# A graph layer whose nodes are reordered so that each lane holds 36 consecutive ones, with column groups of 2048, 2560 and 392

## The chip, the core and the metric

One core of a Trainium2 chip runs the whole program. The metric is the device time of one execution in microseconds. The kernel before takes 252.86 us, the median of three runs (252.83 to 253.35).

## What is computed

```python
h = maximum(layernorm(x), 0)                      # x: 5000 x 64, float32
neighbors = adj @ h                               # adj: 5000 x 5000, float32
neighbors = neighbors / (num_neighbors[:, None] + 1e-7)
out = concat([h, neighbors], -1) @ fc_w.T + fc_b  # fc_w: 64 x 128
return x + relu(out)
```

The matrix adj holds 5000 x 5000 floats, 100 MB, and every element is used once. All else (x, the weights, the result) is 1.28 MB or less apiece.

## The kernel before, in words

The host hands over adj transposed and cut by columns into three tensors, adj_group0 to adj_group2. A row of such a tensor belongs to one source node, a column to one target node. The 5000 nodes are split into 40 tiles of up to 128; 512 nodes (four tiles, RUN) make a block, and lane p of a block holds its nodes 4p to 4p+3, so that one lane's part of a block is contiguous in memory. Nine full blocks (FULL) make 4608 nodes. The other 392 nodes are the tenth block, whose tiles 36, 37 and 38 hold 384 of them for the product, and 8 remaining nodes (REM) go by a small buffer, adj_rem. I write "row t" for the 128 source nodes of tile t: one load of four rows brings 128 lanes x 4 rows x the group's width.

**Prologue.** VectorE and ScalarE normalize x in five sets of eight tiles (normalize, L341 and following; ln_square, ln_std). TensorE turns each set (turn), multiplies it with both halves of the weights (weigh), ScalarE copies the half that adj will multiply into g_sb (copy_g), and VectorE adds the bias to the other half into out_sb (add_bias). Sets 1 to 4 are turned and weighed between products of the first group, at the rows in TURN_AFTER and WEIGH_AFTER.

**The stream.** SyncE's queue issues 35 loads of adj (load, L205 to L212), in order, into one buffer raw of 32768 floats per lane. The first two groups are 2048 columns wide, and their loads of four rows (4.19 MB) go through four slots. The third is 904 wide and uses nine smaller slots of the same buffer. A load waits on the count load_used, which TensorE raises by one after the last product of each load: load n of the wide groups waits until load n-4 has been used. For each row t TensorE multiplies g_sb[t] with the row's columns in two halves of the array at once (multiply, L478 to L486), and sums in PSUM: each bank of acc holds 2 x 512 target nodes, side 0 in lanes 0 to 63, side 1 in lanes 64 to 127. A float32 product is two matmul instructions, so a 2048-wide row is eight of them and a 904-wide row four.

**Counts.** num_neighbors is loaded in nine rows of 512 into every twelfth lane of nn, inverted at full size, and spread to all lanes by one matmul with a one-lane selector (pick) per side and set (spread, L467 to L475), after rows 31 to 35 of the first group. ScalarE copies the result into rnn_bc.

**Between groups.** When a group's sums are complete, VectorE scales them by the counts (scale), TensorE flips them back to node-major form between products of the next group (flip, at FLIP_AFTER), and VectorE adds the self part, applies relu and adds x (finish). ScalarE's queue stores a group's result (store).

**End.** The last group's bank is scaled in two halves, flipped onto a preloaded self part (preload_self, flip_last), finished in two halves (finish_last) and stored: the full block by ScalarE's queue, the last 392 nodes by SyncE's.

```python
if n >= WIDE_SLOTS:
    sp.wait_ge(load_used, loads_before(n))            # SyncE, before the load is issued
```

Of the kernel before, what the change touches and what calls it, by code (L numbers as in the profile page):

```python
# [7 lines left out]
ALU = mybir.AluOpType  # L8
# [8 lines left out]
WIDE_SLOTS = 4  # L17

REM_STEP = 4
NN_STEP = 12  # L20
# [4 lines left out]
P = 1  # L25
GROUPS = [(0, 2048, 0), (2048, 2048, 2), (4096, 904, 4)]
ALIGN = 1

LAST_STEPS = (4, 4, 4, 4, 4, 4, 2, 2, 2, 1)


def gnn_layer(nc, x, adj_groups, num_neighbors, fc_t, fc_b, out):

# [15 lines left out]
    LAST_W = N - TAIL0  # L49
    LAST_LANES = LAST_W // RUN  # L50
    PAD0 = LAST_LANES // 32 * 32
    assert 0 < REM <= 32 and TAIL_RUN == RUN - 1 and TILES % (2 * RUN) == 0 and LAST_W % RUN == 0
    G = len(GROUPS)
    BANKS = TILES // (2 * RUN)
    LAST = BANKS - 1
    BT = 2 * RUN
    WIDE = GROUPS[0][1]
    NARROW = GROUPS[-1][1]
    NARROW_SLOTS = WIDE_SLOTS * WIDE // NARROW

    def banks(g):
        first, w, b0 = GROUPS[g]
        return range(b0, b0 + -(-w // (2 * BLOCK)))

    def sides(g, b):

        first, w, _ = GROUPS[g]
        c = b * 2 * BLOCK - first
        return [(0, c, min(BLOCK, w - c)), (1, c + BLOCK, min(BLOCK, w - c - BLOCK))]
# [3 lines left out]
    for g in range(G):  # L73
        for m in range(FULL + 1):
            n = RUN if m < FULL else TAIL_RUN
            step = RUN if g < G - 1 else LAST_STEPS[m]
            LOADS += [(g, m, i, min(n, i + step)) for i in range(0, n, step)]
    FIRST_LOAD = [[ld[0] for ld in LOADS].index(g) for g in range(G)]
    NARROW0 = FIRST_LOAD[G - 1]

    def slot(n):

        if n < NARROW0:
            return n % WIDE_SLOTS, n % WIDE_SLOTS * RUN * WIDE, n // WIDE_SLOTS
        k = n - NARROW0
        return k % NARROW_SLOTS, k % NARROW_SLOTS * RUN * NARROW, k // NARROW_SLOTS

    def loads_before(n):

        if n < NARROW0:  # L90
            return n - WIDE_SLOTS + 1
        if n - NARROW0 >= NARROW_SLOTS:
            return n - NARROW_SLOTS + 1
        end = slot(n)[1] + RUN * NARROW - 1
        return max(k for k in range(NARROW0) if k % WIDE_SLOTS <= end // (RUN * WIDE) and
                   k % WIDE_SLOTS >= slot(n)[1] // (RUN * WIDE)) + 1

# [3 lines left out]
    SPREAD_AFTER = {(0, 31 + b): b for b in range(BANKS)}  # L101
# [3 lines left out]
    LN_OPS = 9  # L105

    with ExitStack() as ctx:
# [5 lines left out]

        raw = sb("raw", [LANES, WIDE_SLOTS * RUN * WIDE])
        adj_rem = sb("adj_rem", [LANES, WIDE])
# [3 lines left out]
        cen = sb("cen", [LANES, BT, F])  # L119
        h_pairs = [sb(f"h_pairs{i}", [LANES, BT, F]) for i in range(2)]  # L120
        ht = [sb(f"ht{i}", [LANES, BLOCK]) for i in range(2)]
        ht_rows = sb("ht_rows", [LANES, BLOCK])
        rnn_bc = sb("rnn_bc", [LANES, BANKS, RUN, LANES])
        sums = [sb(f"sums{i}", [LANES, RUN, LANES]) for i in range(2)]
        ht_rem = sb("ht_rem", [LANES, LANES])
        nn = sb("nn", [LANES, BLOCK])
        rnn = sb("rnn", [LANES, BLOCK])
        pick = sb("pick", [LANES, 2 * BANKS, HALF])
        w_both = sb("w_both", [2 * F, 2 * F])
        bias = sb("bias", [LANES, F])  # L130
        ident = sb("ident", [LANES, LANES])
        mean = sb("mean", [LANES, BT])
# [5 lines left out]
        acc = [ctx.enter_context(nc.psum_tensor(f"acc{b}", [LANES, BLOCK], F32)) for b in range(BANKS)]  # L138
        turned = ctx.enter_context(nc.psum_tensor("turned", [LANES, BLOCK], F32))
        y = [ctx.enter_context(nc.psum_tensor(f"y{s}", [LANES, BLOCK], F32)) for s in range(2)]  # L140

        x_cleared = sem("x_cleared")
        x_loaded = [sem("x_loaded_first"), sem("x_loaded_rest")]
# [4 lines left out]
        loaded_wide = [sem(f"loaded_wide{s}") for s in range(WIDE_SLOTS)]  # L148
        loaded_narrow = [sem(f"loaded_narrow{s}") for s in range(NARROW_SLOTS)]
# [6 lines left out]
        pad_cleared = sem("pad_cleared")  # L156
        pick_ready = sem("pick_ready")
        rem_cleared = sem("rem_cleared")
        rnn_chain = sem("rnn_chain")
        turned_done = sem("turned_done")  # L160
# [15 lines left out]
        def runs(v, r):  # L176
            return v.rearrange("(p i) f -> p (i f)", i=r)

# [3 lines left out]
        def tile_major(v):  # L182
            return v.rearrange("k (p i) -> k i p", i=RUN)

        def half_runs(v, k):

            return v[:, BT * LAST:TILES, :].rearrange("p (s k i) f -> p k s (i f)", s=2, k=2)[:, k, :, :]

        def half_sides(k):

            return y[k][:, 0:BLOCK // 2].rearrange("p (s j) -> p s j", s=2)
# [4 lines left out]
        def loaded(n):  # L196
            k, _, before = slot(n)
            return (loaded_wide if n < NARROW0 else loaded_narrow)[k], 16 * before + 16

        block = ctx.enter_context(nc.Block())  # L200

        @block.sync
        def _(sp):
            def load(n):
                g, m, i0, i1 = LOADS[n]  # L205
                w = GROUPS[g][1]
                if n >= WIDE_SLOTS:
# [32 lines left out]
        def _(act):  # L240
            def load_rem(g):
                w = GROUPS[g][1]
# [4 lines left out]
                act.dma_start(adj_rem[0:REM * REM_STEP:REM_STEP, 0:w], adj_groups[g][REM0:N, 0:w]  # L247
                              ).then_inc(rem_loaded, 16)
# [8 lines left out]
            def load_counts():  # L257
                act.wait_ge(nn_cleared, 1)
                m = 2 * BANKS - 1
                act.dma_start(nn[0:m * NN_STEP:NN_STEP, :], num_neighbors[0:TAIL0].rearrange("(m n) -> m n", n=BLOCK)  # L260
                              ).then_inc(nn_loaded, 16)
                act.dma_start(nn[m * NN_STEP:m * NN_STEP + 1, 0:LAST_W],
                              num_neighbors[TAIL0:N].rearrange("(m n) -> m n", m=1)).then_inc(nn_loaded, 16)

            def ln_square(b):
                act.wait_ge(ln_dve, LN_OPS * b + 3)
                nc.scalar.activation(out_sb[:, BT * b:BT * (b + 1), :], cen[:], ACT.Square).then_inc(ln_act, 1)  # L267
# [5 lines left out]
            def copy_turned(b):  # L273
# [3 lines left out]
                if b < LAST:  # L277
                    nc.scalar.activation(ht[b % 2][:], turned[:], ACT.Copy).then_inc(turned_copied, 1)  # L278
                else:

                    nc.scalar.activation(tile_major(ht_rows[HALF:LANES, :]),
                                         turned[HALF:LANES, :].rearrange("k (i p) -> k i p", i=RUN), ACT.Copy)

                    p0 = (REM0 - TAIL0) // RUN
                    nc.scalar.activation(
                        ht_rem[HALF:LANES, 0:REM * REM_STEP].rearrange("k (p i z) -> k p i z", i=RUN, z=REM_STEP)[:, :, :, 0],
                        turned[HALF:LANES, :].rearrange("k (i p) -> k p i", i=RUN)[:, p0:LAST_LANES, :], ACT.Copy)
                    nc.scalar.activation(ht[b % 2][:], turned[:], ACT.Copy).then_inc(turned_copied, 1)

            def copy_g(b):  # L290
                act.wait_ge(weighed, b + 1)
                for s in range(2):
                    t0 = BT * b + RUN * s
                    nc.scalar.activation(g_sb[:, t0:t0 + RUN, :],  # L294
                                         y[s][:].rearrange("p (i k) -> p i k", i=RUN)[:, :, F:2 * F],
                                         ACT.Copy).then_inc(g_copied, 1)

            def copy_spread(b):
                act.wait_ge(spread_done, b + 1)
                nc.scalar.activation(rnn_bc[:, b, :, :], tile_major(y[b % 2][:]), ACT.Copy).then_inc(spread_copied, 1)  # L300

            def store(g):
                t0 = banks(g)[0] * BT
                t1 = t0 + len(banks(g)) * BT if g < G - 1 else t0 + RUN
                act.wait_ge(out_ready, banks(g)[-1] + 1)
                act.dma_start(out[t0 * LANES:t1 * LANES, :].rearrange("(m p i) f -> p m (i f)", p=LANES, i=RUN),
# [273 lines left out]
```

## Time and profile before

| | before |
|---|---|
| median of 3 runs | 252.86 us |
| the profiled execution's own time | 253.62 us |
| its span in the profile | 251.8 us |
| adj loads | 35, in all 100 MB |
| mean rate of the DMA engines over the span | 408 GB/s |
| TensorE busy | 202.7 us (80%) |
| VectorE busy | 37.0 us (15%) |
| ScalarE busy | 15.7 us (6%) |

The span runs from the first instruction to the last on the core; the 1.8 us between span and time lie around it. Busy time tells how long an engine had something to do, not that the end waited for it. "DMA share" is the mean busy share of the core's 16 DMA engines in a stretch (values a little over 1 come from how packets are put into the stretches). A timeline row gives start, length, engine, line, output and inputs; what stands in brackets is the idle time before it and what ended it.

### The profile page before, as it was taken

To read this page: it belongs to the slowest core of one execution; us is meant where nothing else is said; L and a number is where in the kernel's file an instruction comes from. 1 tells how busy PE (TensorE), PEld (TensorE's weight loads), DVE (VectorE), ACT (ScalarE), POOL (GpSimd) and SP (SyncE) were. 2 spreads that over 40 slices of the span, in tenths; PEclk is the share of its full clock that TensorE was granted. 3 is DMA by queue.
4 is the path that set the end of the run, shared out by engine and by line. 5 is a ranking of instruction groups with operands and counts; after the bars stand their busy time and mean duration, and the time that the engine had idled before them with its cause. 6 is when DMAs were issued, how large, how long until landed. Compare 5 with 4: busy or idle time off the path is not lost.

```text
span 251.8 us, 2143 instructions
## 1 busy us (share of the span) xinstructions
PE 202.7 (80%) x956; PEld 74.5 (30%) x956; DVE 37.0 (15%) x78; ACT 15.7 (6%) x34; POOL 2.6 (1%) x8
## 2 busy tenths in 40 slices
PE   0409997797696997999599995985866999998994
PEld 0403342332231532333132331221221334443431
DVE  4650063336100010002002200000000001310002
ACT  3210112120120010200000000000000000000000
POOL 4000000000000000000000000000000000000000
PEclk9999999999999999999979998899999999999999
DMA  6899999999999999999999999999999999999971
GB/s 182 365 427 453 432 426 418 422 458 436 422 422 416 437 450 409 450 416 424 442 437 442 428 429 429 432 430 432 428 418 433 415 430 425 434 415 419 422 286 37
DMA packets 8156, 102.80 MB, mean 408 GB/s; under 512 B 1134, under 2 KB 3635, under 8 KB 4804
## 3 DMA queue, kind: packets, MB, share of 16 engines
q1 hardware_dynamic: 6448, 101.22, 94.3%
q10 hardware_dynamic: 1700, 1.46, 1.7%
q8 instruction: 7, 0.11, 0.2%
q14 instruction: 1, 0.01, 0.0%
HBM read 101.40 MB, written 1.28 MB: 408 GB/s over the span
## 4 chain that ended last, share of the span: by engine, by line
DMA 75%; PE 21%; SPq 1%; DVE 1%; issue 0%
DMA raw<-adj_group 75%; PE acc L484 20%; SPq L212 1%; PE acc L494 0%; DVE out_sb L414 0%; PE y L520 0%; SPq L221 0%; PE turned L445 0%; PE y L506 0%; DVE nn L337 0%; DVE sums L398 0%; DVE x_sb L338 0%; DVE warm L336 0%
## 5 line engine op out<-in xcount | busy, mean ns | idle before, releaser
L484 PE MATMUL acc<-raw,g_sb 128*64 128x512 f32 (+1 forms) x780 | 180.6, 601 | 36.0 <-DMA raw<-adj_group 35.8
L484 PEld LDWEIGHTS acc<-raw,g_sb 128*64 128x64 f32 x780 | 59.1, 140 | 146.4 <-issue 97.5
L398 DVE TENSOR_TENSOR sums<-acc,rnn_bc 128x512 f32<-128x512 f32 (+1 forms) x6 | 3.3, 597 | 118.8 <-PE acc L484 118.8
L445 PE MATMUL turned<-ident,h_pairs 128*128 128x128 f32 x20 | 3.7, 315 | 8.7 <-DVE h_pairs L367 8.7
L376 DVE TENSOR_TENSOR out_sb<-y,bias 128x256 f32<-128x256 f32 x10 | 3.8, 419 | 33.1 <-ACT g_sb L294 33.1
L459 PE MATMUL y<-w_both,ht 64*128 64x128 f32 (+1 forms) x80 | 7.6, 317 | 0.8 <-ACT ht L278 0.8
L459 PEld LDWEIGHTS y<-w_both,ht 64*128 64x128 f32 x80 | 6.3, 215 | 4.4 <-issue 4.4
L404 DVE TENSOR_TENSOR out_sb<-y,out_sb 128x512 f32<-128x512 f32 x4 | 2.8, 692 | 30.6 <-PE y L506 30.6
L354 DVE TENSOR_REDUCE var<-out_sb 128x8 f32<-128x512 f32 x5 | 3.4, 686 | 23.2 <-ACT out_sb L267 23.2
L445 PEld LDWEIGHTS turned<-ident,h_pairs 128*128 128x128 f32 x20 | 2.4, 155 | 11.9 <-issue 11.1
L494 PE MATMUL acc<-adj_rem,g_sb 128*64 128x512 f32 (+1 forms) x20 | 5.6, 582 | 0.0
L294 ACT ACTIVATE g_sb<-y 128x256 f32<-128x256 f32 x10 | 3.3, 380 | 32.5 <-PE y L459 19.4
L473 PE MATMUL y<-rnn,pick 128*64 128x512 f32 x20 | 5.1, 592 | 0.0
L300 ACT ACTIVATE rnn_bc<-y 128x512 f32<-128x512 f32 x5 | 3.0, 597 | 17.5 <-PE y L473 17.5
L278 ACT ACTIVATE ht<-turned 128x512 f32<-128x512 f32 x4 | 2.4, 597 | 26.6 <-PE turned L445 26.6
L348 DVE TENSOR_REDUCE mean<-x_sb 128x8 f32<-128x512 f32 x5 | 3.4, 680 | 2.4 <-DMA x_sb<-x 2.4
L352 DVE TENSOR_TENSOR cen<-x_sb,mean 128x512 f32<-128x512 f32 x5 | 3.5, 693 | 0.2
L360 DVE TENSOR_TENSOR cen<-cen,rstd 128x512 f32<-128x512 f32 x5 | 3.5, 692 | 0.2
L267 ACT ACTIVATE out_sb<-cen 128x512 f32<-128x512 f32 x5 | 3.1, 626 | 5.5 <-DVE cen L352 3.6
L385 DVE RECIPROCAL rnn<-nn 128x512 f32<-128x512 f32 x1 | 3.4, 3353 | 0.0
L407 DVE SCALAR_TENSOR_TENSOR out_sb<-out_sb,x_sb 128x512 f32<-128x512 f32 x4 | 2.8, 691 | 0.1
L506 PEld LDWEIGHTS y<-ident,sums 128*128 128x128 f32 x16 | 1.7, 141 | 3.2 <-issue 3.2
(36 smaller groups left out, 28.3 us busy)
## 6 DMA issues: line engine op xcount, KB each, us to landing
raw<-adj_group SPq DMA_DIRECT2D x18, 4096.0 KB, 31.4
raw<-adj_group SPq DMA_DIRECT2D x6, 1808.0 KB, 25.2
raw<-adj_group SPq DMA_DIRECT2D x2, 3072.0 KB, 29.3
raw<-adj_group SPq DMA_DIRECT2D x6, 904.0 KB, 25.4
raw<-adj_group SPq DMA_DIRECT2D x3, 452.0 KB, 17.6
out<-out_sb ACTq DMA_DIRECT2D x2, 512.0 KB, 28.9
x_sb<-x SPq DMA_DIRECT2D x1, 896.0 KB
x_sb<-x SPq DMA_DIRECT2D x1, 256.0 KB, 2.9
```

The costliest lines, as they stand in the source:

```text
L294: nc.scalar.activation(g_sb[:, t0:t0 + RUN, :], y[s][:].rearrange("p (i k) -> p i k", i=RUN)[:, :, F:2 * F], ACT.Copy).then_inc(g_copied, 1)
L348: nc.vector.tensor_reduce(mean[:], x_sb[:, t0:t1, :], AX_X, ALU.add).then_inc(ln_dve, 1)
L352: nc.vector.tensor_tensor(cen[:], x_sb[:, t0:t1, :], bcast(mean[:]), ALU.subtract).then_inc(ln_dve, 1)
L354: nc.vector.tensor_reduce(var[:], out_sb[:, t0:t1, :], AX_X, ALU.add).then_inc(ln_dve, 1)
L360: nc.vector.tensor_tensor(cen[:], cen[:], bcast(rstd[:]), ALU.mult).then_inc(ln_dve, 1)
L376: nc.vector.tensor_tensor(out_sb[:, t0:t0 + RUN, :], y[s][:].rearrange("p (i k) -> p i k", i=RUN)[:, :, 0:F], bias[:].unsqueeze(1).to_broa ...
L385: nc.vector.reciprocal(rnn[:], nn[:]).then_inc(rnn_chain, 1)
L445: last = nc.tensor.transpose(turned[:, i * LANES:(i + 1) * LANES], flat(h_pairs[b % 2][:, 2 * i:2 * i + 2, :]), ident[:])
L459: last = nc.tensor.matmul(y[s][:, c:c + (F if apart else 2 * F)], ht[b % 2][k, c:c + LANES], w_both[k, 0:F if apart else 2 * F], start=Tru ...
L473: last = nc.tensor.matmul(y[b % 2][s * HALF:(s + 1) * HALF, :], pick[:, 2 * b + s, :], rnn[:], start=True, stop=True, tile_position=(0, s ...
L484: last = nc.tensor.matmul(acc[b][s * HALF:(s + 1) * HALF, 0:width], g_sb[:, t, :], raw[:, c + c0:c + c0 + width], start=t == 0, stop=t == ...
L494: last = nc.tensor.matmul(acc[b][s * HALF:(s + 1) * HALF, 0:width], g_sb[:, CH, :], adj_rem[:, c0:c0 + width], start=False, stop=False, ti ...
```

## The change

The host orders the first 4608 nodes otherwise: lane p of the 128 holds the 36 consecutive nodes 36p to 36p+35, and block m takes from lane p the nodes 36p + 9i + m (i = 0 to 3). So x, the counts and the result of these nodes are each one contiguous run per lane. The last 392 nodes are laid out as two sides of 196, two nodes a lane in 98 lanes.

- **x** comes in by one DMA of 9216 bytes per lane and one of 98 lanes x 2 x 512 bytes. Normalizing, adding the bias and finishing read and write strided views of the new order.
- **Groups** are now 2048, 2560 and 392 columns wide. The second has two full banks and one of 2 x 256 columns, the third one bank of 2 x 196 columns, which reuses the PSUM bank named turned.
- **Loads in rings.** Row t of a group stands at place (RING[g][0] + t mod RING[g][1]) times the group's width in raw: 16 rows of 2048, 12 rows of 2560, or rows from place 20 on of 392. A load waits until every earlier load that overlaps its place has been used (loads_before). There are 37 loads. The last one of the first group (load 9, rows 36 to 38) stands at floats 8192 to 14335; the first of the second group (load 10, rows 0 to 3) at 0 to 10239.
- **Counts** are loaded with 36 per lane, inverted at that size, widened to 64 copies each in rnn_wide (VectorE), and spread by matmuls with the identity: 4 of 128 columns per set, and for the last set 12 of 64 or 98 columns.
- **End.** scale_last, flip_last and finish_last work on two pieces of 98 nodes x 2 sides. The bank before it is scaled into a zeroed cen and flipped with a doubled identity (ident_twice).

```diff
-GROUPS = [(0, 2048, 0), (2048, 2048, 2), (4096, 904, 4)]
-LAST_STEPS = (4, 4, 4, 4, 4, 4, 2, 2, 2, 1)
+P = 512
+GROUPS = [(0, 4, 0), (4, 5, 2), (9, 1, 5)]
+STEPS = [(4, 4, 4, 4, 4, 4, 4, 4, 4, 4), (4, 4, 4, 4, 4, 4, 4, 4, 2, 1), (4, 4, 4, 4, 4, 4, 4, 2, 2, 1)]
+RING = [(0, 16), (0, 12), (20, 60)]
...
+    def place(n):
+
+        g, m, i0, _ = LOADS[n]
+        return (RING[g][0] + (m * RUN + i0) % RING[g][1]) * WIDTH[g]
...
     def loads_before(n):
...
+        return max([k + 1 for k in range(n) if place(k) < place_end(n) and place(n) < place_end(k)] + [n - LANDINGS + 1, 0])
...
-    FLIP_AFTER = {(1, 7): 0, (1, 9): 1, (2, 7): 2, (2, 11): 3}
-    PRELOAD_AFTER = (2, 23)
+    FLIP_AFTER = {(1, 7): 0, (1, 9): 1, (2, 9): 2, (2, 13): 3, (2, 17): 4}
+    PRELOAD_AFTER = (2, 25)
...
-            load_x(0, 2).then_inc(x_loaded[0], 16)
-            load_x(2, FULL).then_inc(x_loaded[1], 16)
+            sp.dma_start(flat(x_sb[:, 0:ROWS, :]), x[0:TAIL0, :].rearrange("(p r) f -> p (r f)", r=ROWS)
+                         ).then_inc(x_loaded[0], 16)
...
             def spread(b):
...
-                for s in range(2):
-                    last = nc.tensor.matmul(y[b % 2][s * HALF:(s + 1) * HALF, :], pick[:, 2 * b + s, :], rnn[:],
-                                            start=True, stop=True, tile_position=(0, s * HALF))
+                if b < PAIRS:
+                    for i in range(RUN):
+                        t = i * FULL + 2 * b
+                        last = nc.tensor.matmul(y[b % 2][:, i * LANES:(i + 1) * LANES], flat(rnn_wide[:, t:t + 2, :]),
+                                                ident[:], start=True, stop=True)
...
             def flip_last():
-                for k in range(2):
-                    pe.wait_ge(scaled, LAST + k + 1)
-                    for i in range(2):
-                        last = nc.tensor.matmul(half_sides(k)[:, :, i * F:(i + 1) * F],
-                                                sums[LAST % 2][:, 2 * k + i, :], ident[:], start=False, stop=i == 1)
-                    last.then_inc(flipped, 1)
+                for i in range(2):
+                    pe.wait_ge(scaled, LAST + i + 1)
+                    nc.tensor.matmul(y[i][0:LAST_LANES, 0:2 * F], sums[0][:, i * LAST_LANES:(i + 1) * LAST_LANES],
+                                     ident[:], start=False, stop=True).then_inc(flipped, 1)
```

SyncE's queue before, the loads of x and of adj (sizes are lanes x floats):

```order
L215 DMA x_sb<-x 128x2x256
L215 DMA x_sb<-x 128x7x256
L221 DMA x_sb<-x 98x256 [waits x_cleared]
L212 DMA raw<-adj_group 128x8192 x4
L212 DMA raw<-adj_group 128x8192 [waits load_used] x5
L212 DMA raw<-adj_group 128x6144 [waits load_used]
L212 DMA raw<-adj_group 128x8192 [waits load_used] x9
L212 DMA raw<-adj_group 128x6144 [waits load_used]
L212 DMA raw<-adj_group 128x3616 [waits load_used] x6
L212 DMA raw<-adj_group 128x1808 [waits load_used] x6
L212 DMA raw<-adj_group 128x904 [waits load_used] x3
```

And with the change:

```order
L226 DMA x_sb<-x 128x2304
L229 DMA x_sb<-x 98x2x128 [waits x_cleared]
L224 DMA raw<-adj_group 128x8192 x4
L224 DMA raw<-adj_group 128x8192 [waits load_used] x5
L224 DMA raw<-adj_group 128x6144 [waits load_used]
L224 DMA raw<-adj_group 128x10240 [waits load_used] x8
L224 DMA raw<-adj_group 128x5120 [waits load_used] x2
L224 DMA raw<-adj_group 128x2560 [waits load_used] x3
L224 DMA raw<-adj_group 128x1568 [waits load_used] x7
L224 DMA raw<-adj_group 128x784 [waits load_used] x4
L224 DMA raw<-adj_group 128x392 [waits load_used] x3
```

One load of x is gone, and the adj loads stand one place earlier. The queue is in order: a load that waits holds back all behind it. The first 128x10240 load (load 10) waits for a load_used of 10, that is for the use of the 128x6144 load right before it; before the change it waited for a count of 7.

TensorE from row 31 to row 38 of the first group before (y is the spread counts, acc the sums):

```order
L484 MATMUL acc<-raw,g_sb 64x512 x16
L473 MATMUL y<-rnn,pick 64x512 x2
L484 MATMUL acc<-raw,g_sb 64x512 x4
...
L484 MATMUL acc<-raw,g_sb 64x512 x4
L473 MATMUL y<-rnn,pick 64x512 x2
L484 MATMUL acc<-raw,g_sb 64x512 x8
L494 MATMUL acc<-adj_rem,g_sb 64x512 x4
L484 MATMUL acc<-raw,g_sb 64x512 x36
```

And with the change:

```order
L544 MATMUL acc<-raw,g_sb 64x512 x16
L523 MATMUL y<-ident,rnn_wide 128x128 x4
L544 MATMUL acc<-raw,g_sb 64x512 x4
...
L544 MATMUL acc<-raw,g_sb 64x512 x4
L529 MATMUL y<-ident,rnn_wide 64x64 x4
L533 MATMUL y<-ident,rnn_wide 64x98 x2
L529 MATMUL y<-ident,rnn_wide 64x64 x4
L533 MATMUL y<-ident,rnn_wide 64x98 x2
L544 MATMUL acc<-raw,g_sb 64x512 x8
L555 MATMUL acc<-adj_rem,g_sb 64x512 x4
L544 MATMUL acc<-raw,g_sb 64x512 x8
```

The rows of adj stand as they stood; four spreads are of four narrower matmuls each instead of two, and the fifth is of twelve. (Each of these lines is two instructions in the profile.)

TensorE through the whole last group with the change:

```order
L544 MATMUL turned<-raw,g_sb 64x196 x8
L555 MATMUL turned<-adj_rem,g_sb 64x196 x2
L544 MATMUL turned<-raw,g_sb 64x196 x12
L569 MATMUL y<-ident,sums 128x128 x4
L544 MATMUL turned<-raw,g_sb 64x196 x8
L569 MATMUL y<-ident,sums 128x128 x4
L544 MATMUL turned<-raw,g_sb 64x196 x8
L571 MATMUL y<-ident_twice,cen 128x64 x4
L544 MATMUL turned<-raw,g_sb 64x196 x16
L579 MATMUL y<-out_sb,ident 98x128 x2
L544 MATMUL turned<-raw,g_sb 64x196 x26
L585 MATMUL y<-ident,sums 98x128 x2
```

Before, each of its 39 rows was a 64x512 and a 64x392 product; now each is two of 64x196, and three flips stand among them instead of two.

## Rows read from the trace of the kernel before

**Rows 1.** The page: DMA share and rate by fortieths of the span, and the chain
```profile
DMA  6899999999999999999999999999999999999971
GB/s 182 365 427 453 432 426 418 422 458 436 422 422 416 437 450 409 450 416 424 442 437 442 428 429 429 432 430 432 428 418 433 415 430 425 434 415 419 422 286 37
...
DMA 75%; PE 21%; SPq 1%; DVE 1%; issue 0%
```
**Rows 2.** Stretches at the start: us, busy by engine, TensorE clock, DMA share, GB/s
```profile
1.50:2.00 0.50, 0.00 (x0) 0.00 (x0) 0.43 (x2) 0.50 (x1) 0.50 (x1) 1.00 0.37 47
4.00:4.50 0.50, 0.00 (x0) 0.00 (x0) 0.47 (x2) 0.00 (x0) 0.00 (x0) 1.00 0.92 295
6.50:8.00 1.50, 0.00 (x0) 0.00 (x0) 1.16 (x4) 0.21 (x1) 0.00 (x0) 1.00 0.41 137
8.00:14.00 6.00, 3.17 (x20) 2.53 (x20) 4.04 (x11) 1.99 (x5) 0.00 (x0) 1.00 1.03 439
```
**Rows 3.** Timeline of the start: issues of x and adj, and the first product
```profile
0.74 0.94 SPq L215 DMA_DIRECT2D x_sb<-x  x2
...
0.94 0.48 DVE L337 MEMSET nn<- 128x512 f32 x1
...
1.84 0.73 SPq L221 DMA_DIRECT2D x_sb<-x  x1
2.61 2.91 SPq L212 DMA_DIRECT2D raw<-adj_group  x4
...
19.13 7.17 PE L484 MATMUL acc<-raw,g_sb 128*64 128x512 f32 x24 [6.46 <-DMA raw<-adj_group]
```
**Rows 4.** Timeline of TensorE, from load 7 to the second group
```profile
88.45 7.09 PE L484 MATMUL acc<-raw,g_sb 128*64 128x512 f32 x32 [0.33 <-DMA raw<-adj_group]
...
98.17 1.94 PE L484 MATMUL acc<-raw,g_sb 128*64 128x512 f32 x8 [1.77 <-DMA raw<-adj_group]
99.93 1.03 PE L473 MATMUL y<-rnn,pick 128*64 128x512 f32 x4
100.79 1.89 PE L484 MATMUL acc<-raw,g_sb 128*64 128x512 f32 x8
...
111.95 1.89 PE L494 MATMUL acc<-adj_rem,g_sb 128*64 128x512 f32 x8
113.67 8.75 PE L484 MATMUL acc<-raw,g_sb 128*64 128x512 f32 x40
125.20 3.61 PE L484 MATMUL acc<-raw,g_sb 128*64 128x512 f32 x8 [2.78 <-DMA raw<-adj_group]
```
**Rows 5.** Timeline of TensorE earlier in the first group, a weigh and a turn
```profile
32.38 1.16 PE L459 MATMUL y<-w_both,ht 64*128 64x128 f32 x16
33.47 3.65 PE L484 MATMUL acc<-raw,g_sb 128*64 128x512 f32 x16
...
52.40 0.66 PE L445 MATMUL turned<-ident,h_pairs 128*128 128x128 f32 x4
```
**Rows 6.** Timeline of weight loads, the last rows of adj
```profile
242.47 0.20 PEld L484 LDWEIGHTS acc<-raw,g_sb 128*64 128x64 f32 x4 [1.17 <-DMA raw<-adj_group]
...
244.70 0.20 PEld L484 LDWEIGHTS acc<-raw,g_sb 128*64 128x64 f32 x3 [0.32 <-DMA raw<-adj_group]
...
245.81 0.29 PEld L484 LDWEIGHTS acc<-raw,g_sb 128*64 128x64 f32 x4 [0.57 <-DMA raw<-adj_group]
```
**Rows 7.** Timeline of the end, from the last products to the last store
```profile
242.48 4.50 PE L484 MATMUL acc<-raw,g_sb 128*64 128x512 f32 x20 [0.29 <-DMA raw<-adj_group]
...
247.04 0.76 DVE L398 TENSOR_TENSOR sums<-acc,rnn_bc 128x256 f32<-128x256 f32 x2 [25.86 <-PE acc L484]
247.51 1.16 PE L520 MATMUL y<-ident,sums 128*128 128x128 f32 x8 [0.53 <-DVE sums L398]
248.26 0.87 DVE L414 SCALAR_TENSOR_TENSOR out_sb<-y,x_sb 128x256 f32<-128x256 f32 x2 [0.47 <-PE y L520]
249.16 0.36 SPq L226 DMA_DIRECT2D out<-out_sb  x1
```
**Rows 8.** Groups of VectorE instructions by line and shape: busy us, mean ns
```profile
L385 DVE RECIPROCAL rnn<-nn 128x512 f32<-128x512 f32 x1 | 3.4, 3353 | 0.0
...
L398 DVE TENSOR_TENSOR sums<-acc,rnn_bc 128x512 f32<-128x512 f32 x4 | 2.6, 686 | 92.9 <-PE acc L484 92.9
...
L398 DVE TENSOR_TENSOR sums<-acc,rnn_bc 128x256 f32<-128x256 f32 x2 | 0.8, 419 | 25.9 <-PE acc L484 25.9
```
**Rows 9.** Stretches of ten us in the second group (the clock is the third number from the right)
```profile
120.00:130.00 10.00, 7.22 (x28) 2.07 (x26) 0.00 (x0) 0.00 (x0) 0.00 (x0) 0.83 1.01 436
```
**Rows 10.** The page: weight loads of the adj products, busy us and mean ns
```profile
L484 PEld LDWEIGHTS acc<-raw,g_sb 128*64 128x64 f32 x780 | 59.1, 140 | 146.4 <-issue 97.5
```

More of the change, by code:

```diff
@@ L147, in gnn_layer @@
         bias_loaded = sem("bias_loaded")
-        loaded_wide = [sem(f"loaded_wide{s}") for s in range(WIDE_SLOTS)]
-        loaded_narrow = [sem(f"loaded_narrow{s}") for s in range(NARROW_SLOTS)]
+        landed = [sem(f"landed{k}") for k in range(LANDINGS)]
         rem_loaded = sem("rem_loaded")
@@ L312, in _ @@
             load_weights()
-            for b in range(BANKS):
+            for b in range(SETS):
                 ln_square(b)
@@ L323, in _ @@
                     load_rem(0)
-            copy_g(LAST)
-            for b in range(BANKS):
+            copy_g(SETS - 1)
+            for b in range(SETS):
                 copy_spread(b)
@@ new lines, in scale_alone @@
+            def scale_alone(g):
+                wait_sums(g, ALONE)
+                dve.wait_ge(halves_ready, 2)
+                for s in range(2):
+                    k = slice(s * HALF, (s + 1) * HALF)
+                    last = nc.vector.tensor_tensor(split(cen[k, :])[:, :, s * HALF:(s + 1) * HALF],
+                                                   tile_major(acc[ALONE][k, 0:BLOCK // 2]),
+                                                   split(rnn_bc[k, ALONE, 0:BLOCK // 2]), ALU.mult)
+                last.then_inc(scaled, 1)
@@ L427, in _ @@
             add_bias(3)
+            prepare_halves()
             add_bias(4)
-            for g in range(G - 1):
-                for b in banks(g):
-                    scale(g, b, 0, RUN)
-                for b in banks(g):
-                    finish(b)
-            scale(G - 1, LAST, 0, 2)
-            scale(G - 1, LAST, 2, 4)
+            for b in banks(0):
+                scale(0, b)
+            for b in banks(0):
+                finish(b)
+            scale(1, 2)
+            scale(1, 3)
+            scale_alone(1)
+            for b in banks(1):
+                finish(b)
+            scale_last(2)
             finish_last()
@@ L505, in flip @@
                 for i in range(RUN):
-                    last = nc.tensor.transpose(y[b % 2][:].rearrange("p (s i f) -> p i s f", s=2, i=RUN)[:, i, :, :],
-                                               sums[b % 2][:, i, :], ident[:])
+                    c = slice(i * LANES, (i + 1) * LANES)
+                    if b < PAIRS:
+                        last = nc.tensor.transpose(y[b % 2][:, c], sums[b % 2][:, c], ident[:])
+                    else:
+                        last = nc.tensor.matmul(y[b % 2][:, i * F:(i + 1) * F], cen[:, c], ident_twice[:],
+                                                start=True, stop=True)
                 last.then_inc(flipped, 1)
```

310 lines of the change are left out of this document (166 added, 144 removed).

## The prediction

> **What bounds the kernel now.** I read the page first. Its line by fortieths shows the DMA engines full from the third slice to the thirty-eighth at about 430 GB/s, and the chain that ended last is 75% DMA of adj [rows 1]. So the time is: when the stream of adj starts, the 100 MB at that rate, every moment at which the queue runs dry, and what comes after the last landing. Next the timelines of TensorE: it waits for a landing before nearly every load, starting loads 7 and 8 at 88.45 and 98.17, so one load of 4.19 MB lands each 9.72 us (432 GB/s) [rows 4]. TensorE needs about 7.0 of these 9.72 us for four rows (88.45 to 95.4), so what is added to it is mostly hidden. Exceptions are the places where the stream waits for TensorE. Before, that never empties the queue: three loads are always in flight behind the one in use. Last, the two ends: the start [rows 2, 3] and the tail [rows 6, 7].
>
> **The start.** x is fetched in pieces of 1 KB; these move at 295 GB/s from 4.0 to 4.5 us, and from 6.5 to 8.0 all traffic is down to 137 with the engines 41% busy; from 8.0 they are full [rows 2]. The first product starts at 19.13, one load's 9.72 before that is 9.4: this is when the latest DMA engine began on adj [rows 3]. The mean one began near 8.2. With the change x is 1.18 MB in pieces of 9 KB and 0.1 MB in pieces of 512 bytes. At 430 GB/s that is 3.0 us from the first packets at about 1.8 [rows 2], so 4.8; the weights' packets add some tenths. SyncE issues one DMA less (0.47 us) and VectorE's clearing of nn (0.48) no longer stands ahead of the clearing of x, so adj is issued at about 2.0 instead of 2.61 [rows 3] and is ready behind x. I take 5.2 for the mean engine and, with the same spread of 1.2, 6.4 for the latest: **-3.0 us**. Bounds: -0.6 (only the earlier issue counts) and -4.4 (every engine starts at 5.0). TensorE doesn't take this back: set 0 no longer has a small load of its own and waits for all of x, till about 5, but now TensorE idles 6.46 us before load 0 [rows 3].
>
> **The join of the first two groups.** Load 10 is the first of width 2560. Its place, floats 0 to 10239, overlaps load 9's, 8192 to 14335, and so SyncE may issue it only when load_used is 10. Load 9 is the last of the first group, and loads 11 and 12 stand behind load 10 in the queue. So after load 9 has landed nothing of adj is in flight until TensorE has used it. Before, load 9 landed at about 98.17 + 3/4 x 9.72 = 105.5. TensorE was then still in load 8's rows, since rows 32 to 35 each have a spread of 0.86 us behind them (99.93 to 100.79) and the remainder takes 1.72 us (111.95 to 113.67). Row 38 ran from 113.67 to 115.4 [rows 4]. So TensorE is done **9.9 us** after the landing. This was free with three loads in flight; that cover is now gone.
>
> To it come the changed spreads. Spreads 1 to 3 are eight instructions of 128 columns each. A turn's four take 0.6 us, so 1.2 for eight, and a weigh's sixteen take 1.09 (32.38 to 33.47), so 0.55 for eight [rows 5]. I take 1.0, +0.15 each. The last spread is 24 instructions of 64 or 98 columns: at the weigh's 0.068 us each 1.64, at the turn's 0.15 each 3.6. I take 1.75, since their columns are fewer: +0.9. Together +1.35, bounds 0 and 4.
>
> From issue to first packets: x is issued at 0.74 and the first 47 GB/s show in the stretch from 1.5 to 2.0 [rows 2, 3], which is 1.1 us; bounds 0.8 and 1.5. The gap is 9.9 + 1.35 + 1.1 = **+12.4 us**, bounds 10.7 and 15.4. The page "DMA: Bandwidth & Descriptors" of the Trainium skill (Latency and other measured facts) has about 0.6 us to the first byte for such queues; by that the sum would be 0.5 less. The trace has the longer time, and I keep it.
>
> **After the gap** the stream is as long as before: 51.1 + 7.8 MB against 40.9 + 18.1 MB. A load of 5.24 MB takes 12.1 us, and TensorE's four rows of 2.5 bank pairs at 0.86 (2 of them are 1.72) take 8.6. Loads 13 on wait for the load three before, so at least one whole load is always in flight. The third group's places are free once row 33 of the second is used; no second gap. TensorE idles some 13 us in the gap. After 2.78 us idle its eight instructions took 3.61 us instead of 1.9, and the granted clock of that stretch is 0.83, so for part of it the engine was at the lower level, 1.2 GHz [rows 4, 9]. The page "TensorE: Matmul & The Clock Gate" of the Trainium skill (The HAM clock gate) says that an idle array falls to half its clock; the trace agrees. Ten us at 0.83 cost 1.7 us, and load 10 has 3.5 to spare: nothing on the path.
>
> The second group's store grows by 128 KB; in pieces near 1 KB that is 0.4 us at 295 GB/s [rows 2]: **+0.4**, bounds 0 and 0.9. The counts' small packets and the remainder's finer ones I cost at nothing: under 0.1 MB, bounded by that 0.9.
>
> **The last group and the tail.** A row's four instructions of 196 columns: from 512 columns at 0.43 us a pair, 0.33; with the weigh's overhead up to 0.39. The 39 rows are 12.9 to 15.2 us, with remainder, three flips and preload about 2.7, and 2.15 for the second group's last row before them: 17.8 to 20.1. The DMAs have 7.83 MB, 18.2 us, and a store of 655 KB, 2.2 us: 20.4. TensorE just keeps up, and I add 0.3 for it. After the last landing TensorE now works from 245.81 to 247.0 [rows 6, 7]; then 0.5: -0.65. From 247.04 to 249.13 it is scale, flip, finish in two halves [rows 7]. A scale of 256 elements takes 419 ns and one of 512 686 [rows 8], so 1.04 ns each, and 98 take 254: two are 0.5, the last flip some 0.35, the last finish 0.29, with the handing over 1.22 instead of 2.09: -0.85. The last store is the same. Together **-1.2 us**, bounds -2 and +0.5.
>
> VectorE's added work (rnn_wide, about 2.7 us at 2560 elements, the cleared cen, ident_twice) falls where it idles for tens of us before the first scale; the full-size inversion of 3.4 us [rows 8] goes from the same place. Both cost nothing.
>
> **Sum.** -3.0 + 12.4 + 0.4 - 1.2 = +8.6 us. The profiled execution took 253.62 (span 251.8, 1.8 around it), so 262.2 in its terms; it was 0.76 above the median, and against the median of 252.86 it is **261.5 us**. This case has a chance of 0.90, and its own range is 258.2 to 264.6.
>
> **Rivals.**
> - *No gap, the other side.* If load 10 were released while load 9 is still coming in, as now, the start and the tail remain: 252.86 - 3.0 + 0.4 - 1.2 = 249.1 us. What decides is the time from load 9's landing to its use: below 2.7 us (with the 1.1 us of restart, the 3.8 that is saved) the change wins. For it: DMA engines end unevenly, so some idle less. Against: 9.9 us in the trace, and an overlap that stands in the numbers. 0.03, and 0.02 for a gap so short that both cancel (252.9).
> - *TensorE bounds the last group.* If weight loads of 0.14 us [rows 10] can't overlap under so short products, a row takes 0.56, and 21.8 + 2.7 + 2.15 = 26.7 us stand against 20.4: 267.5 us. Against: the weigh has as many weight loads and takes 0.068 per instruction [rows 5]. 0.04.
> - *Small transfers bound it.* The last group comes in 14 loads of 0.2 to 0.8 MB. If each paid the 1.1 us of start by itself, 15.4 us: 276.9. The trace speaks against it: loads of 0.46 MB land 1.11 us apart (244.70, 245.81), 417 GB/s [rows 6]. 0.01. The page "DMA: Bandwidth & Descriptors" of the Trainium skill (Bandwidth) has 341 GB/s at 1 MB and asks for at least that; at this rate, an estimate, the group would take 4.8 us more, but its figure is for a transfer alone, and the row is of queued ones.
>
> **Numbers.** What a measurement of this kernel tells from no change is about 0.2%, 0.5 us. Slower by more: 0.95; within: 0.02; faster: 0.03. The range for 8 in 10 is the forecast's own widened a little for bounds that add up: 258.0 to 265.0.
>
> **What would show it.** A stretch of about 12 us near 103 to 115 with a DMA rate near zero, and TensorE idle for some 13 us before load 10; TensorE's first adj product near 16 instead of 19.13; landings of the second group 12.1 us apart without a pause; the last landing near 255; about 4.4 us from there to the end of the span. I am wrong if the rate doesn't drop at the join, if it drops again later, or if TensorE in the last group never waits for a landing.

## The result, and the profile after

The changed kernel takes **265.73 us** (median of 4 runs, 265.50 to 266.27) against 252.85 before: 1.052 times as long, 95% interval 1.0502 to 1.0538. Forecast were 261.5 us and a range of 258.0 to 265.0. The direction and the place of the loss were right, the time lies 0.7 us above the range. The profiled execution took 265.64 us with a span of 263.9, 12.0 more than before's 253.62.

The page of the changed kernel, the lines that answer to [rows 1] (PEclk is the clock granted to TensorE, in tenths):

```profile
PEclk9999999999999999995569999997979997999999
DMA  7999999999999994039999999999999999999992
GB/s 279 400 441 385 438 417 441 428 422 446 407 442 427 435 416 205 2 112 422 460 410 447 447 397 456 435 420 410 456 440 428 405 430 419 427 421 421 418 398 79
```

The hole in the DMA lines is the join of the first two groups; nothing like it stands anywhere else. The timeline of TensorE there, answering to [rows 4]:

```profile
97.00 1.94 PE L544 MATMUL acc<-raw,g_sb 128*64 128x512 f32 x8 [1.53 <-DMA raw<-adj_group]
98.86 1.16 PE L523 MATMUL y<-ident,rnn_wide 128*128 128x128 f32 x8
99.95 1.94 PE L544 MATMUL acc<-raw,g_sb 128*64 128x512 f32 x8
...
112.11 2.16 PE L555 MATMUL acc<-adj_rem,g_sb 128*64 128x512 f32 x8
113.82 2.16 PE L544 MATMUL acc<-raw,g_sb 128*64 128x512 f32 x8
130.90 11.63 PE L544 MATMUL acc<-raw,g_sb 128*64 128x512 f32 x48 [14.91 <-DMA raw<-adj_group]
143.03 7.52 PE L544 MATMUL acc<-raw,g_sb 128*64 128x512 f32 x40 [0.50 <-DMA raw<-adj_group]
```

SyncE's queue in the same stretch, and the DMA engines by stretches (columns as in [rows 2]):

```profile
116.02 1.28 SPq L224 DMA_DIRECT2D raw<-adj_group  x3
```
```profile
95.00:100.00 5.00, 3.47 (x23) 1.77 (x21) 0.00 (x0) 0.60 (x1) 0.00 (x0) 1.00 0.98 419
...
105.00:110.00 5.00, 5.00 (x47) 3.41 (x48) 0.00 (x0) 1.15 (x2) 0.00 (x0) 1.00 0.00 0
...
116.50:117.50 1.00, 0.00 (x0) 0.00 (x0) 0.81 (x2) 0.00 (x0) 0.00 (x0) 1.00 1.75 492
117.50:119.00 1.50, 0.00 (x0) 0.00 (x0) 0.00 (x0) 0.00 (x0) 0.00 (x0) 1.00 0.36 109
119.00:125.00 6.00, 0.00 (x0) 0.00 (x0) 0.00 (x0) 0.00 (x0) 0.00 (x0) 0.55 1.01 437
```

By the landing events of the trace, load 9 lands at 104.23 us and load 10 at 130.85. Row 38, the last of load 9, ends at 116.0; in the same moment SyncE issues loads 10, 11 and 12 at once. From 105 to 115 the DMA engines move nothing but one packet of 16 KB (instructions).

The start, answering to [rows 2, 3]: timeline of TensorE, and stretches.

```profile
25.00 2.08 PE L506 MATMUL y<-w_both,ht 64*128 64x128 f32 x16 [12.42 <-DMA w_both<-fc_t]
27.93 8.49 PE L544 MATMUL acc<-raw,g_sb 128*64 128x512 f32 x32 [0.85 <-ACT g_sb L303]
```
```profile
4.00:5.00 1.00, 0.00 (x0) 0.00 (x0) 0.00 (x0) 0.00 (x0) 0.00 (x0) 1.00 1.03 433
...
8.00:20.00 12.00, 1.09 (x4) 0.71 (x4) 5.90 (x14) 2.16 (x5) 0.00 (x0) 1.00 1.03 438
20.00:27.00 7.00, 2.00 (x16) 1.79 (x16) 0.00 (x0) 0.00 (x0) 0.00 (x0) 1.00 0.95 382
```

x comes faster (433 GB/s from 4 to 5 us; before it was 295 from 4.0 to 4.5), but TensorE's first product of adj is at 27.93, not near 16: it waits for the weights, which have landed at 24.95. And from 20 to 27 us the stream runs at 382 GB/s. Load 0 lands at 16.95, 2.1 us earlier than before (19.04), load 9 only 1.2 earlier (104.23 against 105.43).

The end, answering to [rows 7]:

```profile
255.73 4.53 PE L544 MATMUL turned<-raw,g_sb 128*64 128x196 f32 x52
260.31 0.42 DVE L439 TENSOR_TENSOR sums<-turned,rnn_bc 128x98 f32<-128x98 f32 x2 [7.00 <-PE turned L544]
260.63 0.68 PE L585 MATMUL y<-ident,sums 128*98 128x128 f32 x4 [0.36 <-DVE sums L439]
261.12 0.51 DVE L456 SCALAR_TENSOR_TENSOR out_sb<-y,x_sb 98x128 f32<-98x128 f32 x2 [0.39 <-PE y L585]
261.66 0.36 SPq L233 DMA_DIRECT2D out<-out_sb  x1
```

The last load lands at 259.39 and the span ends 4.5 us later, instead of 6.0 us. The last 13 rows run without a wait.

So the 12.1 us between the two spans are, going by when the last of the 16 DMA engines has landed its part of a load: -1.2 at the start, +14.5 for the gap (26.62 from landing to landing, less 12.13 for load 10 itself), +0.3 for the stream behind it (128.5 us to the last landing), -1.5 for the tail.

### The profile page after: what moved, and what is told of

Same layout as the page of the kernel before. It is cut to its first block, busy times and chain, and to the rows that moved or that the text cites. A ratio compares the mean times of both kernels' runs of the same rounds, so it can differ in the third digit from the quotient of the medians.

```text
span 263.9 us, 2548 instructions
## 1 busy us (share of the span) xinstructions
PE 203.5 (77%) x1156; PEld 89.2 (34%) x1156; DVE 35.9 (14%) x80; ACT 15.2 (6%) x35; POOL 3.0 (1%) x8
## 4 chain that ended last, share of the span: by engine, by line
DMA 51%; PE 47%; ACT 1%; DVE 0%; issue 0%; SPq 0%
DMA raw<-adj_group 42%; PE acc L544 36%; DMA w_both<-fc_t 9%; PE turned L544 5%; PE y L506 2%; PE y L523 1%; PE turned L493 1%; PE acc L555 1%; PE y L569 0%; PE y L571 0%; ACT L318 0%; PE y L529 0%; ACT g_sb L303 0%; PE y L579 0%; DVE out_sb L456 0%
## 5 line engine op out<-in xcount | busy, mean ns | idle before, releaser
L544 PE MATMUL acc<-raw,g_sb 128*64 128x512 f32 (+1 forms) x780 | 166.1, 579 | 33.5 <-DMA raw<-adj_group 32.5
L506 PE MATMUL y<-w_both,ht 64*128 64x128 f32 (+1 forms) x80 | 7.6, 317 | 12.4 <-DMA w_both<-fc_t 12.4
L544 PE MATMUL turned<-raw,g_sb 128*64 128x196 f32 x156 | 14.2, 332 | 0.0
L544 PEld LDWEIGHTS turned<-raw,g_sb 128*64 128x64 f32 x156 | 10.8, 137 | 2.2 <-issue 0.3
L448 DVE TENSOR_TENSOR out_sb<-y,out_sb 128x512 f32<-128x512 f32 (+1 forms) x5 | 3.2, 638 | 45.5 <-PE y L569 44.4
L523 PEld LDWEIGHTS y<-ident,rnn_wide 128*128 128x128 f32 x32 | 3.9, 191 | 3.2 <-issue 3.2
L523 PE MATMUL y<-ident,rnn_wide 128*128 128x128 f32 x32 | 4.6, 288 | 0.0
L373 DVE TENSOR_REDUCE var<-sums 128x8 f32<-128x512 f32 x5 | 3.4, 686 | 8.6 <-ACT sums L277 8.6
L362 DVE TENSOR_REDUCE mean<-x_sb 128x8 f32<-128x512 f32 (+1 forms) x6 | 3.5, 590 | 5.1 <-DMA x_sb<-x 5.1
L369 DVE TENSOR_TENSOR cen<-x_sb,mean 128x512 f32<-128x512 f32 (+1 forms) x6 | 3.5, 602 | 0.2
L277 ACT ACTIVATE sums<-cen 128x512 f32<-128x512 f32 x5 | 3.1, 625 | 7.2 <-DVE cen L369 5.9
```

Of the source, the lines that this page charges most:

```text
L362: last = nc.vector.tensor_reduce(narrow(mean[:]), rows, AX_X, ALU.add)
L369: last = nc.vector.tensor_tensor(wide(cen[:]), rows, m.unsqueeze(len(m.shape)).to_broadcast(list(rows.shape)), ALU.subtract)
L373: nc.vector.tensor_reduce(var[:], sums[0][:].rearrange("p (t f) -> p t f", f=F), AX_X, ALU.add).then_inc(ln_dve, 1)
L448: nc.vector.tensor_tensor(o, split(y[b % 2][:, 0:RUN * F * (m1 - m0)]), o, ALU.add).then_inc(summed, 1)
L506: last = nc.tensor.matmul(y[s][:, c:c + (F if apart else 2 * F)], ht[b % 2][k, c:c + LANES], w_both[k, 0:F if apart else 2 * F], start=Tru ...
L523: last = nc.tensor.matmul(y[b % 2][:, i * LANES:(i + 1) * LANES], flat(rnn_wide[:, t:t + 2, :]), ident[:], start=True, stop=True)
```

## The experiments

Each is an edit of the changed kernel or of e1_ring_phase, except e2_before_with_wait. Ratios are to the kernel before, run on the same chip at the same time, whose medians were 253.06, 252.81 and 252.84 us. Their 95% intervals reach 0.1 to 0.45% to either side, so a difference of half a microsecond between two experiments is not resolved. What is read from a trace (landings, starts, packets) is one execution each.

**e1_ring_phase: the same ring, turned.**

```diff
-        return (RING[g][0] + (m * RUN + i0) % RING[g][1]) * WIDTH[g]
+        return (RING[g][0] + (m * RUN + i0 + PHASE[g]) % RING[g][1]) * WIDTH[g]
+PHASE = [8, 0, 0]
```

> The changed kernel with one edit: the first group's ring is turned by 8 rows, so that its last load stands at floats 24576 to 30719 and load 10 waits for a count of 8 instead of 10. Theory A (the gap between the groups is the cost: from load 9's landing at 104.23 us to load 10's at 130.85 are 26.6 us, of which 12.1 are the load itself): the 14.4 us go, time 265.7 - 14.4 = 251.3 us, landings at the join about 12 us apart. Rival B (40 KB pieces or the new widths make the stream slower, and the gap hides part of it): only part goes, 254 to 258 us, with slower landings in the second group. Rival C (without the rest of the gap TensorE in the last group becomes the bound): 253 to 256, and TensorE ends later than 0.6 us after the last landing.

Measured: **250.59 us**, ratio to before 0.9896 (0.9861 to 0.9931). The gap is gone, and load 10 lands at 116.20, 12.1 us after load 9 (104.08). The second group lands as theory A says, and the time is 0.7 us below A's 251.3; B falls. C falls by its time, though its sign is there: TensorE ends at 245.4, 1.6 us after the last landing at 243.7, see e6_ring_steps. Its DMA line and the timeline at the join:

```profile
DMA  8998999999999999999999999999999999999991
```
```profile
113.64 2.16 PE L545 MATMUL acc<-raw,g_sb 128*64 128x512 f32 x8
116.25 8.81 PE L545 MATMUL acc<-raw,g_sb 128*64 128x512 f32 x48 [0.44 <-DMA raw<-adj_group]
128.69 1.97 PE L545 MATMUL acc<-raw,g_sb 128*64 128x512 f32 x4 [3.63 <-DMA raw<-adj_group]
```

TensorE's work on load 9 ends where it ended in the changed kernel; only nobody waits for it now.

**e2_before_with_wait: the wait alone, in the kernel before.**

```diff
     def loads_before(n):
+        if n == 10:
+            return 10
```

> The kernel before with one edit: load 10 waits for a count of 10 instead of 7. Theory A: the wait alone makes the loss. Load 9 lands at 105.4 and is used at 115.4, restart 1.2 us to the first packets, which are slow (2.3 instead of 1.5 us each in the changed kernel, here perhaps 2.0 instead of 1.2), so +12 us: 265 us. If the restart's extra time depends on the piece (32 KB here, 40 KB there), the gap beyond TensorE's 10 us is 0.3 us or more shorter than the 2.9 us of the changed kernel. Rival B: +8 us or less, since loads 11 and 12 come right behind and a burst catches up.

Measured: **266.0 us**, 1.0507 (1.0466 to 1.0548). One changed wait makes the old kernel as slow as the changed one, +13 us. No burst catches up; B falls. The restart (the table below) is 0.4 us shorter here than with the larger pieces, as the expectation allowed for; these are two single traces. SyncE and TensorE there:

```profile
114.85 1.87 SPq L214 DMA_DIRECT2D raw<-adj_group  x4
```
```profile
126.85 9.04 PE L486 MATMUL acc<-raw,g_sb 128*64 128x512 f32 x32 [12.04 <-DMA raw<-adj_group]
```

**e3_spreads_later: less for TensorE between landing and release.**

```diff
-    SPREAD_AFTER = {(0, 31 + b): b for b in range(SETS)}
+    SPREAD_AFTER = {(1, b): b for b in range(SETS)}
```

> The changed kernel with one edit: the five spreads of the counts are done after rows 0 to 4 of the second group instead of rows 31 to 35 of the first. TensorE then has nothing but adj rows between the landing of load 8 (96.95) and the use of load 9, except the remainder. Theory A (the gap is TensorE's time from landing to use, plus a fixed restart): four spreads between load 8's landing and load 9's use go, 3 x 1.0 + 0.9 + some tenths; TensorE is at load 9 as it lands, 104.3 + 5.15 + 1.7 = 111.2 instead of 115.7: -4.5 us, 261.2 us. Rival B (the gap is set by something else than TensorE): no change, 265.7.

Measured: **261.29 us**, 1.0334 (1.0291 to 1.0377); -4.4 against the changed kernel. SyncE issues load 10 at 111.30, and TensorE gets it 15 us later:

```profile
111.30 1.28 SPq L224 DMA_DIRECT2D raw<-adj_group  x3
```
```profile
126.24 4.11 PE L544 MATMUL acc<-raw,g_sb 128*64 128x512 f32 x10 [14.98 <-DMA raw<-adj_group]
```

**e8_phase_four: a release in between.** PHASE = [4, 0, 0] instead of [8, 0, 0].

> As e1_ring_phase, but the first group's ring is turned by 4 rows instead of 8, so that load 10 overlaps loads 7 and 8 and waits for a count of 9: the use of load 8, which e1_ring_phase's timeline has at about 108.7 us, 4.6 us after load 9's landing (104.1). Theory A (a gap costs what lies between the last landing and the release, plus 2.7 us from issue to a full stream): load 10 lands at 108.7 + 2.7 + 12.1 = 123.5 instead of 116.2, +7.3 us, 257.9 us. Rival B (only the wait counts, the restart overlaps): +4.6, 255.2 us. Rival C (any empty queue costs the whole 14 us): 265.

Measured: **257.81 us**, 1.0189 (1.0165 to 1.0213). B and C fall by their times. The sum of A is right, its two parts less so, and they cancel by luck: load 8 is released at 107.72, a microsecond earlier than I had written (I had counted the last spread, which comes behind it), and load 10 lands at 123.69, a restart of 3.8 instead of 2.7. That 3.8 is one DMA engine: the other fifteen have landed their parts by 122.44, which is a restart of 2.6, and one comes 1.25 us behind them. One packet of instructions (16 KB, 0.9 us) lies within load 10, at 112.34; that it is what held this engine up is likely, but the trace does not name the engines.

The four gaps side by side. Landings and issues are the trace's; the restart is the time from the issue of load 10 to its landing, less the load itself at 432 GB/s:

| | load 9 landed | load 10 issued | load 10 landed | landing to issue | restart |
|---|---|---|---|---|---|
| changed | 104.23 | 116.02 | 130.85 | 11.8 | 2.7 |
| e2_before_with_wait (4.19 MB) | 104.65 | 114.85 | 126.81 | 10.2 | 2.3 |
| e3_spreads_later | 104.13 | 111.30 | 126.20 | 7.2 | 2.8 |
| e8_phase_four | 104.11 | 107.72 | 123.69 | 3.6 | 3.8 (2.6 on fifteen engines) |

**e7_x_in_kb: x in pieces of 1 KB again**, on e1_ring_phase.

```diff
-            sp.dma_start(flat(x_sb[:, 0:ROWS, :]), x[0:TAIL0, :].rearrange("(p r) f -> p (r f)", r=ROWS)
-                         ).then_inc(x_loaded[0], 16)
+            for s in range(2):
+                sp.dma_start(x_sb[:, 0:ROWS, :].rearrange("p (c r) f -> p c (r f)", r=RUN)[:, s::2, :],
+                             x[0:TAIL0, :].rearrange("(p c r) f -> p c (r f)", c=FULL, r=RUN)[:, s::2, :]
+                             ).then_inc(x_loaded[0], 16)
```

> As e1_ring_phase, with one edit: x comes in by two DMAs of pieces of 1 KB, 5 and 4 per lane, instead of one of 9 KB per lane, as in the kernel before. Theory A (x in large pieces lets adj begin 2.2 us earlier on the mean DMA engine, 6.0 instead of 8.4, but lets the weights trickle in late, which costs 0.9 by 28 us): load 0 lands 2 us later, load 8 about 1.2 later, time 251.8. Rival B (the earlier start is lost again altogether before the last landing, since one DMA engine is late by then for other reasons): 250.6.

Measured: **252.10 us**, 0.9978 (0.9966 to 0.9990): 1.5 us more than e1_ring_phase by the medians, 2.1 by the ratios. Load 0 lands at 19.68 instead of 16.73, load 8 at 98.47 instead of 96.77, TensorE starts at 19.72. A holds, B falls. So the one DMA of large pieces is worth 1.5 to 2 us, with the price of the late weights already in it. It is worth this in two ways that the edit doesn't separate: larger pieces, and one DMA less ahead of adj, which is issued at 1.70 instead of 2.54.

**e4_ring_weights: the weights on SyncE's queue**, behind x and ahead of adj (same two DMAs, issued there), on e1_ring_phase.

> As e1_ring_phase, and the two loads of the weights are issued by SyncE's queue right behind x, ahead of adj, instead of by ScalarE's. Theory A (the weights' 256-byte packets on the other queue take turns with 32 KB packets of adj, one for one, and so land at 24.95 us, and TensorE starts at 27.9): TensorE's first adj product comes at about 17.5, as load 0 lands. If the slower adj packets between 21 and 27 us (1.4 instead of 1.21 us) come from these too, the time falls by 0.6 us against e1_ring_phase, to 250.7. Rival B (those slow packets have another cause, and TensorE's early start is hidden): no difference to e1_ring_phase.

Measured: **252.12 us**, 0.9969 (0.9952 to 0.9986), slower than e1_ring_phase by 1.5. The cause that A names for TensorE's late start holds, the time doesn't follow. Stretches of this run, and TensorE's first product:

```profile
5.50:7.00 1.50, 0.00 (x0) 0.00 (x0) 0.26 (x1) 0.00 (x0) 0.00 (x0) 1.00 0.27 72
...
20.00:27.00 7.00, 7.00 (x30) 2.12 (x28) 0.00 (x0) 0.00 (x0) 0.00 (x0) 1.00 0.97 417
```
```profile
19.56 5.01 PE L545 MATMUL acc<-raw,g_sb 128*64 128x512 f32 x16 [3.86 <-DMA raw<-adj_group]
```

TensorE no longer waits for weights, and 20 to 27 us is at 417 GB/s instead of 377 in e1_ring_phase. But between x and adj the DMA engines fall to 27% busy: adj, issued from 3.22 on instead of 1.7, isn't there yet. Load 0 lands at 19.51, 2.8 later. In the changed kernel's trace the taking of turns can be counted: from 8 to 20 us the DMA engines start 158 packets of 256 bytes and 159 of adj.

**e5_bias_first: the bias issued ahead of the weights**, on e1_ring_phase.

> As e1_ring_phase (250.6 us), with one edit: ScalarE's queue issues the bias ahead of the weights. In the changed kernel adj moves at 386 GB/s or so between 21 and 27 us, and that is when the bias comes in behind the second half of the weights. Theory A (the bias' packets, all of which read one 256-byte row, slow adj): the bias now comes before adj, the dip goes or moves to where the bias is, and if it goes the time falls by 0.7 us to 249.9. Rival B (any small packets on a second queue slow adj): the dip stays somewhere before 30 us, time 250.6.

Measured: **252.33 us**, 0.9986 (0.9967 to 1.0005), slower than e1_ring_phase by 1.7, by the ratios 2.3. The time decides nothing between the theories, since adj starts late (a hole at 22% busy from 5.5 to 7.0 us), though nothing on SyncE's queue was changed; load 0 lands at 19.06. The trace speaks for A, the bias. The weights still come late here, at 30.24, beside adj; yet from 20 to 27 us the rate is 408 GB/s (26 small packets beside 87 of adj), and from load 0's landing to load 9's it is 86.3 us, as in the kernel before (86.4), where the changed kernel and e1_ring_phase take 87.3. A 32 KB packet of adj takes 1.24 us on the mean from 20 to 27 us here, 1.29 and 1.32 in those two. In the changed kernel's own trace it took 1.23 from 8 to 20, beside as many small packets of the weights. How the bias slows adj stays open; its price in the changed kernel is 0.8 to 0.9 us, from 382 against 433 GB/s over 7 us.

**e6_ring_steps: smaller loads where TensorE falls behind**, on e1_ring_phase; the second group's entry of STEPS is (4, 4, 4, 4, 4, 4, 2, 2, 2, 1).

> As e1_ring_phase, with one edit: the second group's loads are of two rows from row 24 on instead of from row 32 on. Theory A (TensorE bounds the end: it starts load 17, four rows, only as that has landed whole, at 203.2 us, and from there works without a wait to 245.4, 1.6 us after the last landing; part of it at the lower clock): with loads of two rows it starts 6 us earlier there, and ends 0.6 us after the last landing: -1.0 us, 249.6 us. Rival B (the DMA engines bound the end and TensorE's lateness is harmless): no change, 250.6, or +0.2 for two more loads.

Measured: **251.09 us**, 0.9948 (0.9929 to 0.9967). TensorE now does wait for the last landings:

```profile
244.16 0.55 PE L545 MATMUL turned<-raw,g_sb 128*64 128x196 f32 x4 [0.69 <-DMA raw<-adj_group]
245.12 0.55 PE L545 MATMUL turned<-raw,g_sb 128*64 128x196 f32 x4 [0.40 <-DMA raw<-adj_group]
```

Yet nothing is won, and A falls; by the ratios the run is 1.3 us slower than e1_ring_phase (the two intervals just touch), by the medians 0.5; B had +0.2 at most. The last load lands at 245.1 instead of 243.7. Of these 1.4 us 0.6 stand already at load 9 (104.66 against 104.08), before the edit acts; where the other 0.8 come from no run shows. What the trace does show is that TensorE and the latest DMA engine end within a microsecond or two of each other, so that freeing one leaves the other.

## Why the prediction was right or wrong

**The join: right in its mechanism, and undersized by 2.1 us** (14.5 measured, 12.4 forecast). The step "SyncE may issue load 10 only when load_used is 10, nothing of adj is in flight until then" is shown by four runs: removed (e1_ring_phase), put alone into the old kernel (e2_before_with_wait), shortened by work (e3_spreads_later) and by place (e8_phase_four). Of its terms:
- *TensorE from landing to use*, forecast 9.9 + 1.35 = 11.25: measured 11.8. The first part is 10.2 by e2_before_with_wait, which has the old spreads: I had given row 38 the 1.72 us from one row to the next, but SyncE issues 1.93 us after its start (112.92 to 114.85). The changed spreads are then 1.6 instead of 1.35: 1.09 us each instead of the 1.0 I took, the last one 1.3 instead of 1.75, and, which I left out, 0.1 to 0.15 us on each row of adj between full-width spreads (99.95 to 101.82, 1.87 us, against 1.72 before).
- *From issue to a full stream*, forecast 1.1: measured 2.7. **This step failed.** I took the time to the first packets, bounds 0.8 and 1.5, but what counts is when the landing comes. The first packets do start 0.9 us after the issue, at 116.96 (0.9 to 1.0 in all four gaps), and the last engine's at 117.65, after 1.6. But each engine's first packet takes long, 1.8 to 2.7 us instead of 1.51, so that no engine starts a second before 119.16 (the stretches above: a packet counts where it starts). From the end of the last packet to its landing event it is another 0.3 us. On the last engine to start this is 1.6 + 0.8 + 0.3 = 2.7. Why the first packets are slow no run shows. The page of before had the right row, which I read and didn't use:

```profile
x_sb<-x SPq DMA_DIRECT2D x1, 256.0 KB, 2.9
```

The first load of x takes 2.9 us from issue to landing, of which 0.6 are its bytes at 432 GB/s. That is 2.3, what e2_before_with_wait then measured.

**The start: -3.0 forecast, -1.2 measured. This step failed too.** The gain of the large pieces is real, 1.5 us or more by e7_x_in_kb. I took 9.4 to 6.4 for the latest engine; load 0 says 7.2 (16.95 less 9.7). I had x done at 4.8, from the first packets and its bytes; it lands at 6.45, 5.7 us after its issue, so here too the delay of the first packets and the bytes were not the whole. Then 0.9 more was lost by load 9, since the weights and behind them the bias came in among adj's packets, and with the bias the rate fell (e5_bias_first). In the kernel before they came among x's small ones: the weights had landed at 7.2. I had dismissed them as "some tenths" on the path, and wrote that TensorE "doesn't take this back" without looking at what else weigh(0) waits for: it started at 27.93, not near 16. That lateness itself cost nothing, it had caught up by load 8 (1.53 us idle before 97.00). Nor are all -1.2 the change's: the profiled execution of before was 0.76 us above its median. e2_before_with_wait, which has the prologue of before, lands load 9 at 104.65, and against that the start gains only 0.4. With x in pieces of 1 KB the new kernel starts later than the old one (load 0 at 19.68 in e7_x_in_kb, at 19.04 and 18.16 in the two profiles with the old prologue); what in the new prologue takes back part of the gain no run isolates.

**The tail and the last group: -1.2 forecast, -1.5 measured.** The chain behind the last product was sized right: 260.31 to 261.63 is 1.32 us, forecast 1.22. "TensorE just keeps up" was half right. From the second group's last landing at 239.62 it needed 20.6 us, above my 17.8 to 20.1. A row takes 0.35 us, inside my bounds; most of the excess comes from before: it entered the group at 243.4, 3.8 us after that landing instead of 2.15, since it starts on load 17 only as its four rows have landed whole, with part of the next 5 us at the lower clock (0.80 granted from 220 to 225). So my test "wrong if TensorE in the last group never waits" came out against me. It cost 0.4 us in the changed kernel (TensorE ends 0.88 us after the last landing, where I had 0.5), and the 0.3 that I had added for it nearly covers that. The rival's mechanism, weight loads that don't overlap, is refuted by the 0.35 us, where it needed 0.56.

**The clock** fell as said: the granted clock is 0.50 of full (1.2 GHz) from 120 to 125 us, while TensorE idles for 14.9 us. Load 10's 48 instructions took 11.63 us against 8.81 in e1_ring_phase, 2.8 more where I had 1.7. TensorE still had to wait 0.50 us for load 11: covered, as forecast.

**The sum.** 8.6 us were forecast: -3.0, +12.4, +0.4, -1.2. Measured between the profiles: -1.2, +14.5, +0.3, -1.5, 12.1 us. Both misses point the same way. The gap of 14.5 and the start of -1.2 each lie within the bounds that I gave them; only the restart (1.5 at most) lay outside its own. My range let one of them be as bad but not both. The medians differ by 12.9, 0.8 more than the profiles, because the profiled execution of before was 0.76 us above its median; with 0.4 for the start instead of 1.2 the terms give the 12.9.

**The version to keep** is e1_ring_phase. It has all that the change brings but the gap, and is 1% faster than the kernel before. The change as a whole was worth about -2.5 us (250.59 against 253.06), and one overlap of 2048 floats per lane (8192 to 10239) turned it into +12.9.

## What to carry to other kernels

Where a ring's geometry changes between stages, work out for every load which use it waits for and how many bytes are still in flight at that moment; a stream-bound kernel loses from the last landing to the release, plus a restart. Take the restart from a row of a load issued into empty queues, issue to landing less its bytes, not from the first packets. And when the start of the stream is pulled forward, look at what small transfers used to hide in the time before it.

## What was not expected of the hardware

- Restarting the stream costs 2.3 to 2.8 us beyond the bytes in three runs, and in the fourth 2.6 on fifteen engines and 3.8 on the last, though the loads behind are issued at once. The first packet of each engine takes 2.3 us on the mean instead of 1.51 (40 KB).
- Small transfers on a second queue land late beside large pieces, since the two queues take turns packet by packet (158 small ones beside 159 of adj from 8 to 20 us): 256-byte rows of weights issued at 0.9 us landed at 25. In four other runs with these queues unchanged it was 17.5 to 24.9, in the kernel before 7.2.
- The bias behind the weights goes with a slower stream: 382 GB/s from 20 to 27 us instead of 433. The weights alone don't do this (e5_bias_first). Why isn't settled.
- The order of small DMAs on ScalarE's queue moved the start of adj on SyncE's: with the bias first, load 0 landed at 19.06 instead of 16.73 (e5_bias_first). Why isn't settled.
